# Chunk counts of the experts packed into six words and kept in TensorE's registers (cross-attention and MoE block)

## What is computed

```python
logits = x @ gate_w
topk_ids = jnp.argmax(logits, axis=-1)
scores = jax.nn.sigmoid(jnp.max(logits, axis=-1))[:, None]
xs = x * scores
tokens_per_expert = jnp.zeros((E,), jnp.int32).at[topk_ids].add(1)
order = jnp.argsort(topk_ids)
g = ragged_dot(xs[order], routed_gate_w, tokens_per_expert)
u = ragged_dot(xs[order], routed_up_w, tokens_per_expert)
d = ragged_dot(silu(g) * u, routed_down_w, tokens_per_expert)
out = x + swiglu_shared(x) + d[argsort(order)]
```

## Time and profile before

| what | value |
|---|---|
| median of 3 runs | 292.94 us (292.06 to 293.19) |
| the profiled execution's own time | 291.1 us |
| its span, first to last instruction | 289.2 us |
| TensorE matmul busy | 250.5 us, 87% |
| VectorE busy | 163.1 us, 56% |
| ScalarE, GpSimd busy | 94.0 us and 87.9 us |
| mean granted TensorE clock | 0.972 |
| bytes moved by DMA | 68.69 MB, mean 238 GB/s |

### The profile page before, as it was taken

The page is one execution under the profiler, slowest core; times in us unless marked ns, Lnnn a source line. Parts: engine busy times, 40 slices in busy tenths (PEclk is TensorE's granted clock), DMA queues, the critical chain, the costliest instruction groups (busy, mean ns, idle before and its releaser), DMA issues.

```text
span 289.2 us, 12925 instructions
## 1 busy us (share of the span) xinstructions
PE 250.5 (87%) x4627; PEld 184.6 (64%) x4629; DVE 163.1 (56%) x490; ACT 94.0 (33%) x284; POOL 87.9 (30%) x248
## 2 busy tenths in 40 slices
PE   4997899997799899998979999999999999698800
PEld 3765666553375358856867888788788787543700
DVE  0655796878469543016656667666666667424333
ACT  2344875454230110235323333334333333211000
POOL 1262221111005777102222223222222222103772
PEclk9996899999999999999999999999999999999985
DMA  6999994000001325401998869999999999733565
GB/s 196 328 394 410 404 401 157 2 2 1 2 0 37 109 96 165 160 16 50 329 390 286 300 236 331 358 410 415 416 410 411 415 412 409 312 83 94 174 214 164
DMA packets 32559, 68.69 MB, mean 238 GB/s; under 512 B 3966, under 2 KB 18715, under 8 KB 32539
## 3 DMA queue, kind: packets, MB, share of 16 engines
q1 hardware_dynamic: 25723, 61.60, 56.4%
q0 software_dynamic: 1536, 4.20, 4.7%
q10 hardware_dynamic: 5280, 2.62, 3.5%
HBM read 59.49 MB, written 8.91 MB: 237 GB/s over the span
## 4 chain that ended last, share of the span: by engine, by line
PE 66%; DMA 9%; DVE 8%; issue 5%; POOL 5%; ACT 3%; POOLq 1%; SPq 1%; ACTq 1%; DVEq 0%
PE bank L1039 23%; PE bank L961 14%; PE bank L1061 11%; DMA ring_gu<-n_L_ffn_routed_up_w_dram 5%; PE bank L973 5%; POOL xs_flat L463 5%; PE bank L874 3%; PE bank L926 2%; PE bank L909 2%; DMA slot_rows<-late 2%; DVE h_place L531 1%; ACT h_place L749 1%; DVE h_place L532 1%; DMA h_place<-in_L_xattn_kernel_q_dram 1%; DMA xs_flat<-slot_rows,slot_i 1%
## 5 line engine op out<-in xcount | busy, mean ns | idle before, releaser
L1039 PE MATMUL bank<-ring_gu,x_c 128*32 128x128 f32 x2528 | 86.8, 275 | 6.6 <-issue 2.6
L1039 PEld LDWEIGHTS bank<-ring_gu,x_c 128*32 128x32 f32 x2528 | 64.8, 109 | 20.3 <-issue 8.1
L1061 PE MATMUL bank<-ring_d,h_place 128*32 128x128 f32 x1264 | 51.8, 274 | 2.3 <-issue 1.6
L646 DVE TENSOR_TENSOR h_place<-h_place,bank 128x128 f32<-128x128 f32 x79 | 31.2, 395 | 33.2 <-PE bank L1039 30.9
L456 POOL COPY x_c<-xs_flat 128x32 f32 x79 | 16.6, 210 | 101.2 <-PE bank L1039 88.5
L1061 PEld LDWEIGHTS bank<-ring_d,h_place 128*32 128x32 f32 x1264 | 36.1, 109 | 7.7 <-DVE h_place L651 5.3
L792 ACT COPY late<-bank 128x128 f32 (+1 forms) x79 | 21.0, 266 | 57.5 <-PE bank L1061 57.5
L973 PE MATMUL bank<-shd,h_place 128*128 128x256 f32 x128 | 28.4, 380 | 2.1 <-DVE h_place L532 2.1
L651 DVE STREAM_TRANSPOSE h_place<-h_place 128x128 f32<-128x128 f32 x79 | 24.6, 311 | 9.9 <-PE bank L1061 1.7
L787 ACT ACTIVATE h_place<-bank 128x128 f32<-128x128 f32 x79 | 21.9, 277 | 23.6 <-PE bank L1039 19.3
L531 DVE SCALAR_TENSOR_TENSOR h_place<-h_place,bank 128x512 f32<-128x512 f32 x16 | 11.0, 686 | 32.5 <-ACT h_place L749 32.5
(11 more groups left out here) (132 smaller groups left out, 261.9 us busy)
## 6 DMA issues: line engine op xcount, KB each, us to landing
ring_gu<-L_ffn_routed_gate_w_dram SPq DMA_DIRECT2D x32, 512.0 KB, 9.4
ring_gu<-n_L_ffn_routed_up_w_dram SPq DMA_DIRECT2D x32, 512.0 KB, 10.3
ring_d<-L_ffn_routed_down_w_dram SPq DMA_DIRECT2D x32, 512.0 KB, 10.3
slot_rows<-late ACTq DMA_DIRECT2D x10, 256.0 KB, 6.5
x<-in_x_dram SPq DMA_DIRECT2D x4, 512.0 KB, 7.3
slot_rows<-zeros SPq DMA_DIRECT2D x1, 2048.0 KB, 20.4
late<-sorted_rows SPq DMA_DIRECT2D x8, 256.0 KB, 3.4
out_dram<-x SPq DMA_DIRECT2D x8, 256.0 KB, 2.4
```

The source lines that it names most:

```text
L646: v.tensor_tensor(h_r.rearrange("p (m f) -> p m f", m=KF), g_silu.rearrange(rows, m=KF), bank[1][:, 0:P].rearrange(rows, m=KF), ALU.mult). ...
L1039: ins = te.matmul(bank[g][q * LW:(q + 1) * LW, 0:P], x_c[:, k], ring_gu[:, s, g, k, q * P:(q + 1) * P], start=(k == 0), stop=(k == KD - 1))
L1061: ins = te.matmul(bank[2][r:r + LW, 0:DH], hT[:, f * LW:(f + 1) * LW], ring_d[:, s, f, a * DH:(a + 1) * DH], start=(m == 0), stop=(m == HA ...
```

## The change

VectorE gets ten more instructions behind the table `turn` and ahead of the two residuals. They take the numbers of chunks less one of the experts 1 to 30, as five rounds of six, and pack them by shifts and ors into six words of five 6-bit fields (`stream`). TensorE loads the six words into registers between the last four groups of transposes. In the routed stage `next_expert` takes the lowest field of its slot's register, adds it to the running end, and shifts the register; nothing is loaded from SBUF there any more. The last expert's end is `n_chunks + 1`, which is in a register already. The load of the first expert's end ahead of the loop stays.

```diff
+    FIELD = (T // LW - 1).bit_length()
...
+        fields = sb("fields", [1, ROUNDS, RING], I32)
+        stream = sb("stream", [1, RING], I32)
...
             v.tensor_scalar(turn[:, 1:NE + 1], chunk_cum[0:1], 1.0, None, ALU.add).then_inc(table_ready, 1)
 
+            step(v.tensor_scalar(fields.rearrange("p r s -> p (r s)"), chunk_i[0:1, 1:1 + ROUNDS * RING], 1, None, ALU.subtract))
+            step(v.tensor_copy(stream[:], fields[:, ROUNDS - 1]))
+            for r in range(ROUNDS - 2, -1, -1):
+                step(v.tensor_scalar(stream[:], stream[:], FIELD, None, ALU.logical_shift_left))
+                step(v.tensor_tensor(stream[:], stream[:], fields[:, r], ALU.bitwise_or))
+            dve.sem_inc(stream_ready, 1)
+
             shared_residual(0)
             shared_residual(1)
...
             te.matmul(bank[1][0:1, 0:P], begin_f[:], ident[:], start=True, stop=True).then_inc(begin_done, 1)
+
+            slot_end = [pe.alloc_register(f"slot_end{s}") for s in range(RING)]
+            streams = [pe.alloc_register(f"stream{s}") for s in range(RING)]
+            pe.wait_ge(stream_ready, 1)
             for u in range(SORTED_RING, NU):
                 sorted_transposes(u)
+                for s in range(RING):
+                    if s % (NU - SORTED_RING) == u - SORTED_RING:
+                        packed = nc.values_load(
+                            stream[0:1, s:s + 1], engines=(mybir.EngineType.PE,), min_val=0, max_val=(1 << 31) - 1,
+                            skip_runtime_bounds_check_because="masked to the fields")
+                        pe.reg_mov(streams[s], packed & ((1 << FIELD * ROUNDS) - 1))
...
-            def next_expert(w, e, s, landed):
+            def next_expert(w, s, landed, end=None):
 
                 n = (s + 1) % RING
                 pe.wait_ge(gu_in[n], 2 * landed)
                 gate_up(w, n)
-                end = turn_of(e + 2)
+                if end is None:
+                    counts = pe.snap(streams[s], min_val=0, max_val=(1 << FIELD * ROUNDS) - 1)
+                    pe.reg_mov(slot_end[s], w + counts % (1 << FIELD) + 1)
+                    pe.reg_mov(streams[s], counts >> FIELD)
+                    end = pe.snap(slot_end[s], min_val=2, max_val=MAX_CHUNKS + 1)
                 down_of(w, s)
                 return w, end
```

More of the change, by code:

```diff
@@ L258, in build_cross_attention_moe @@
         begin_done = sem("begin_done")
+        stream_ready = sem("stream_ready")
         sortedT_done = sem("sortedT_done")
@@ L1107, in _ @@
                     other_chunks(w, end, s, 16 * it + 16)
-                    w, end = next_expert(end, RING * it + s, s, 16 * it + (16 if s + 1 < RING else 32))
+                    w, end = next_expert(end, s, 16 * it + (16 if s + 1 < RING else 32))
                 carry(w, end)
@@ L1113, in _ @@
                 if s + 1 < REST:
-                    w, end = next_expert(end, RING * ROUNDS + s, s, 16 * ROUNDS + 16)
+                    w, end = next_expert(end, s, 16 * ROUNDS + 16, n_chunks + 1)
             down_of(n_chunks + 1, REST - 1)
```

## The result

The changed kernel takes 296.53 us (median of 20 runs, 294.43 to 299.21), the kernel before 293.09 us beside it on the same chip (20 runs). The ratio is 1.0144 with a 95% interval of 1.0117 to 1.0171, or +4.2 us (3.4 to 5.0). The forecast was +0.65 us, and its range ended at 295.6 us.

What follows compares the result with a forecast made beforehand. Transfers were taken to bound the kernel from 186 us, so the end moves with TensorE reaching chunk 34. 1.65 + 0.2 - 1.2 + 0 = +0.65 us on 292.94 gave 293.6 us, range 291.4 to 295.6 us.

Steps and rivals of the forecast that it cites:

- What bounds the kernel: Routed stage: transfers bind from 186 us, so the end moves with TensorE reaching chunk 34; later gains yield nothing.
- Part one: Ten VectorE instructions ahead of the residuals: TensorE restarts later, +1.65 us, bounds 1.4 to 2.0.
- Nothing absorbs the shift: Between TensorE's restart and the routed stage: no wait takes up the +1.65 us delay from VectorE.
- the sum: All four parts together: 1.65 + 0.2 - 1.2 + 0 = +0.65 us.
- Part two: Six register loads on TensorE between the last transposes: +0.2 us taken, from 0 to 2.2.
- Loads of 0.5 to 0.8 us: Rival, ahead of the routed stage: dear loads cost 0.8 to 2.2 us there; chance 0.2 with dear divisions.
- the rival's 295.4 to 296.8 us: Rival, TensorE's loads and edges: dear loads and divisions, edges gain nothing, +2.45 to +3.85 us; chance 0.2.
- Part three: Nine edges between experts up to chunk 32: 0.13 us gained at each, -1.2 us, ends 0 and 2.25.
- Part four: TensorE's 1.59 us stall at chunk 10, first round: taken as unchanged, 0, ends -1.6 and +1.6.
- the load was the stall: Rival, chunk 10: the 1.59 us stall goes with the load, -0.95 us or 292.0 us; chance 0.22.
- A second stall: Rival, routed stage: moved code brings another stall of 1.6 us, +2.25 us or 295.2 us; chance 0.08.

Runs made afterwards that it cites:

- before: The kernel without the change, first profile: profiled execution 291.1 us; its timed runs beside the changed kernel had a median of 293.09 us.
- after: The changed kernel, against the kernel before: 296.53 us, ratio 1.0144; its first profiled execution took 297.69 us.
- pack_late: Changed kernel with the ten packing instructions moved behind VectorE's half of the shared products: 293.39 us, ratio 1.0054 to the kernel before.
- pad_16: Kernel before plus 17 semaphore increments on TensorE ahead of the routed stage, nothing else changed: 293.67 us, ratio 1.0058.
- fill_idle: Changed kernel plus three unused 128x512 matmuls in TensorE's idle time behind the packing: 293.58 us, ratio 1.0030 to the kernel before.
- pack_only: Kernel before plus the ten packing instructions on VectorE, words unread, TensorE's program as before: 296.1 us, ratio 1.0118.
- fill_2: Second profile of fill_idle, nothing changed: profiled execution 296.22 us.
- after_again: Second profile of the changed kernel, nothing changed: profiled execution 293.42 us, without the lower clock behind the restart.
- before_4: Fourth profile of the kernel before, nothing changed: profiled execution 291.95 us.
- late_pad208: pack_late plus 208 semaphore increments at the start of TensorE's program: ratio 1.1037 to the kernel before.
- after_4: Fourth profile of the changed kernel, nothing changed: profiled execution 300.09 us.

## Why the prediction was wrong

**What bounds the kernel: right.** The end moves with chunk 34. Against before, chunk 34 and the last gate product moved by 5.02 and 5.52 in after, 1.44 and 1.46 in pack_late, 0.88 and 0.81 in pad_16, 3.13 and 3.49 in fill_idle, 10.35 and 10.12 in pack_only. The twenty later edges are shorter too in the kernels with the words, and it yields nothing.

**Part one, "+1.65 us": the step that failed.** The ten instructions cost 1.88 us, a size within its bounds of 1.4 to 2.0. What failed is the sentence that followed the shift to the routed stage: "Nothing absorbs the shift". It is true and not all. The text expected an idle time near 2.8 us and priced it at its length. The idle time came at 3.28 us, and with it in five profiles of six a stretch of 3.4 or 6.8 us at 1.2 GHz, which takes another 1.7 to 2.8 us. Neither the sum, its bounds nor a rival had this. That it is the idle time, and not the work on VectorE, is shown by fill_idle and fill_2 (same VectorE, filled, no fall) and pack_late (same work elsewhere, no fall). By times, the packing alone costs +3.5 us (1.9 to 5.0) where 1.65 stood; by the medians of all runs +3.1.

**Part two, "+0.2 us": near.** About 0.40 us in all profiles with the loads and no fall (33.58 to 33.62 us from restart to stage, against 33.20 to 33.22). "Loads of 0.5 to 0.8 us" is refuted: that would have been 0.8 to 2.2 us. That the rival's 295.4 to 296.8 us hold the measured 296.53 is luck. Of the two figures of the Trainium skill set beside it, the one in Runtime: NRT & Kernel Launch fits; the sum it left unchanged was nearer than the one that the 600 ns of DMA: Bandwidth & Descriptors gave.

**Part three, "-1.2 us": right.** The median edge went from 1.63 to 1.49 us, nine times 0.14 or 1.3 us; the eight edges up to chunk 32 without the stall give 1.2 us together in after_again and 1.3 in after. The bundle with a remainder and a shift hides.

**Part four, "0": right about the load, short about the code.** The rival "the load was the stall" (0.22) is refuted: every kernel without the load has it. "A second stall" didn't come. But the stall is not unchanged. It stays at instruction 2506 while the code shifts under it, out of the gap behind the gate product and into it. Chunk 10 then takes its stall and 0.5 to 0.6 us on top (after 4.35 - 1.48 - 2.28 = 0.59, after_again 0.57, pad_16 0.47; before 0.03), since the six or seven last products come behind the stall and the down product behind them. pad_16, which has nothing but this, measured +1.7 us (0.6 to 2.8) by its ratio and +0.6 by the medians of all runs; the rows show only the half microsecond.

**The sum anew.** From ratios: packing and clock +3.5 (pack_only), code place +1.7 (pad_16), loads +0.4, edges -1.3, together +4.3 us, against +4.2 measured. From the medians of all runs: 3.1 + 0.6 + 0.4 - 1.3 = +2.8 us, against +3.4. From rows alone, an estimate: the shift 1.88, the clock 1.5 (the mean of the four profiles of after: 1.7, 0, 1.7 and 2.7), the loads 0.4, the place of the stall 0.5, the edges -1.3, together +3.0 us. The same from ratios without the packing gives +0.8 for pack_late, measured +1.6 (0.3 to 2.9). The intervals are each more than 1.5 us wide, so the closeness of the totals shows the order of the terms and no more. What the forecast lacked is, by the rows, first the clock behind the idle time (1.5 us) and then the stall's new place (0.5 us).

**Open.** Why the fetch is late at this block and hidden at most others. Why the stall's length varies: the transfer of the instruction queue that ends it begins anywhere from 2.2 us before the stall (before_4) to 1.2 us after the stall's start (late_pad208); what makes it begin late was not found. Whether the place of the code costs more than the half microsecond that the rows show. Why the clock falls behind one idle time of 1.74 or 3.3 us and not behind the next of the same length, and whether the fall 20 us ahead of the restart makes the one at the restart more or less likely. The timed runs of pack_late have a mean clock of 0.9622, nearer to after's 0.9608 than to the 0.9675 of the kernel before beside them, though its profile shows no fall at the restart or behind the stall. It has the one behind the 1.74 us, as most have; where the falls of the other runs lie wasn't traced.

## What to carry to other kernels

Work put ahead of a waiting TensorE costs its length and, once the idle time grows from about 1 to over 3 us (1.7 us was enough at another place), in most executions a stretch at half the clock behind it: put small bookkeeping where TensorE isn't waiting, or give TensorE something to do in the meantime. A microsecond gained in a loop counts only up to the point from which the transfers set the end. And before a change of 0.5% is believed or blamed, run the old kernel with its code shifted by as many instructions, and look at the medians of all runs too: here that alone gave +0.6% by the ratio and +0.2% by the medians.

## What the hardware showed that I had not expected

- TensorE's granted clock fell behind an idle time of 3.2 to 3.3 us in five profiles of six, behind one of 1.74 us in 14 of 20, and behind one of 0.6 to 1.2 us at the restart in none of 14. Behind the stalls of 1.0 to 1.6 us in the first round it never fell (seven), behind those of 2.0 us and more in 11 of 14 (not in pack_late with 3.19, pad_16 with 2.12 and after_4 with 2.00).
- A block of code ends at a fixed instruction. Crossing it at 2506 in the first round cost 1.0 to 3.2 us in 19 profiles and 0.26 us in one, with the weight transfers running (DMA share 1.01 in after's window from 150 us). Behind the first round no stall of over 0.9 us without a recorded cause was seen.
- 48 to 208 semaphore increments in a row at the start of TensorE's program moved the stage by 0.10 to 0.17 us for each (one profile of each length), though the engine has to wait for its data there. The 17 of pad_16 ahead of the stage moved it by nothing (33.22 us from restart to stage, as before).
- Small integer operations of one partition and six elements on VectorE that wait for each other follow at 0.18 to 0.24 us.
